# One transformer layer with eight experts: invert, broadcast and scale one half of the heads one step sooner on VectorE, in five passes

## The reference

```python
x = L0_attn_in_features
mod = (_silu(L0_c) @ L0_wmod).reshape(L0_c.shape[0], 6, 1, -1)
...
h = _layernorm(x, axis=-1) * (1 + ca) + sa
x = x + ga * _L0_attn_ref(h, ...)            # 16 heads, causal
h = _layernorm(x, axis=-1) * (1 + cb) + sb
x = x + gb * _L0_ffn_ref(h, ...)
# inside _L0_ffn_ref
p = jax.nn.softmax(att, axis=-1)             # 32 heads, no mask
o = jnp.einsum('bhqk,bkhd->bqhd', p, v).reshape(B, S, D) @ wo + x
h = jax.nn.gelu(jnp.einsum('metd,edf->metf', xe, w1) + b1[None, :, None, :], approximate=False)
y = jnp.einsum('metf,efd->metd', h, w2) + b2[None, :, None, :]
```

## Time and profile before

| | us |
|---|---|
| median of 3 runs | 1638.02 (1637.07 to 1643.39) |
| the profiled execution | 1635.07 |
| its span, first to last instruction | 1633.3 |
| PE busy | 1456.5 (89%) |
| DVE busy | 1181.6 (72%) |
| ACT busy | 997.7 (61%) |
| POOL busy | 528.7 (32%) |

### The profile page before, as it was taken

How to read it: one execution, slowest core, us unless ns; L and a number is a source line. 1 busy time by engine, 2 the same in 40 slices (tenths; PEclk the granted TensorE clock), 3 DMA queues, 4 the chain that set the end, 5 groups by cost and what they waited for, 6 DMA issues and landing times.

```text
span 1633.3 us, 29723 instructions
## 1 busy us (share of the span) xinstructions
PE 1456.5 (89%) x9637; PEld 614.1 (38%) x9637; DVE 1181.6 (72%) x2891; ACT 997.7 (61%) x2075; POOL 528.7 (32%) x1218
## 2 busy tenths in 40 slices
PE   6685879988999989999899989999899979998987
PEld 4232423333434334343334334343343424343425
DVE  6567589778687776868777786878778587867620
ACT  1152557755667656776567756676577756776761
POOL 4232335245342333414343243414243133312100
PEclk9698899999999999999999999999999999999999
DMA  6851434555344452645345362554336242533111
GB/s 188 211 131 40 130 108 138 125 148 160 92 145 127 135 135 85 185 123 164 95 122 167 95 177 82 164 148 147 89 100 193 76 109 63 161 93 86 60 59 65
DMA packets 158749, 200.96 MB, mean 123 GB/s; under 512 B 24640, under 2 KB 109952, under 8 KB 158600
## 3 DMA queue, kind: packets, MB, share of 16 engines
q1 hardware_dynamic: 152712, 194.69, 42.1%
q10 hardware_dynamic: 5888, 4.37, 1.0%
HBM read 122.25 MB, written 75.58 MB: 121 GB/s over the span
## 4 chain that ended last, share of the span: by engine, by line
PE 62%; DVE 12%; ACT 7%; DMA 6%; issue 6%; SPq 4%; POOL 2%; POOLq 0%; ACTq 0%; DVEq 0%
PE bank_out L1456 15%; PE bank_scores L1437 11%; PE bank_max L1407 8%; PE bank_side L1370 6%; PE bank_side L1540 5%; DVE neg_max L1681 5%; PE bank_side L1380 3%; PE bank_max L1524 3%; DMA q_stack<-max_parts 3%; ACT probs L1228 3%; PE bank_side L1505 2%; DVE bank_max L1678 2%; PE bank_side L1494 2%; PE bank_side L1524 2%; PE bank_scores L1524 2%
## 5 line engine op out<-in xcount | busy, mean ns | idle before, releaser
L1228 ACT ACTIVATE probs<-bank_scores 128x512 f32<-128x512 f32 (+3 forms) x1536 | 752.4, 543 | 334.0 <-PE bank_scores L1437 324.8
L1681 DVE TENSOR_REDUCE neg_max<-bank_max 128x1 f32<-128x512 f32 x1024 | 654.4, 683 | 123.8 <-PE bank_max L1407 120.6
L1407 PE MATMUL bank_max<-k_stack,q_stack 64*128 64x512 bf16 (+3 forms) x2048 | 318.2, 347 | 74.9 <-DVE neg_max L1681 39.6
L1456 PE MATMUL bank_out<-probs,v_tile 128*9 128x512 f32 (+4 forms) x3072 | 369.3, 553 | 7.1 <-ACT out_raw L1243 2.9
L1437 PE MATMUL bank_scores<-q_stack,k_stack 64*128 64x512 bf16 (+3 forms) x2048 | 318.0, 347 | 43.0 <-ACT probs L1228 34.6
L1678 DVE CUSTOM_DVE_ANT_0 bank_max<-bank_max,causal 128x384 f32<-128x384 f32 (+3 forms) x512 | 241.7, 514 | 113.5 <-PE bank_max L1407 111.2
L1437 PEld LDWEIGHTS bank_scores<-q_stack,k_stack 64*128 64x128 bf16 x2048 | 81.3, 93 | 367.7 <-issue 341.1
L1078 POOL CAST max_parts<-max_row 16x128 bf16<-16x128 f32 x96 | 28.0, 292 | 526.1 <-DVE max_row L1692 526.1
L1407 PEld LDWEIGHTS bank_max<-k_stack,q_stack 64*128 64x128 bf16 x2048 | 104.6, 95 | 159.8 <-issue 91.3
L1540 PE MATMUL bank_side<-w_out,hidden_T 128*128 128x256 f32 x512 | 141.4, 402 | 3.1 <-issue 1.1
L1096 POOL TENSOR_SCALAR_AFFINE_SELECT probs<-probs 128x512 f32<-128x512 f32 x128 | 81.3, 635 | 116.3 <-ACT probs L1228 116.2
(11 more groups left out here) (154 smaller groups left out, 1452.3 us busy)
## 6 DMA issues: line engine op xcount, KB each, us to landing
q_stack<-q_parts SPq DMA_DIRECT2D x124, 256.0 KB, 4.7
k_stack<-k_parts SPq DMA_DIRECT2D x122, 192.0 KB, 6.3
out_raw<-out_raw SPq DMA_DIRECT2D x70, 256.0 KB, 2.0
w_in<-in_L_ffn_w_dram SPq DMA_DIRECT2D x16, 1024.0 KB, 5.2
w_out<-in_L_ffn_w_dram SPq DMA_DIRECT2D x16, 1024.0 KB, 6.1
q_parts<-partsq SPq DMA_DIRECT2D x32, 384.0 KB, 3.1
k_parts<-partsk SPq DMA_DIRECT2D x32, 384.0 KB, 3.3
q_parts<-partsq SPq DMA_DIRECT2D x32, 256.0 KB, 3.2
```

The costliest lines, as they stand in the source:

```text
L1228: nc.scalar.activation(probs[s % 2][:, head_at(k), q0:S], region[bank][:, q0:S], ACT.Exp, scale=float(WIDTH[a]) ** -0.5).then_inc(drained[ ...
L1407: ins = pe.matmul(region[to][:, 0:keys], q_stack[buf][rows, at, qt * P:(qt + 1) * P], k_stack[buf][rows, at, 0:keys], start=(i == 0), stop ...
L1456: ins = pe.matmul(outb[32 * k:32 * k + WIDTH[a] + 1, q0:S], v_tile[a][:, kt, g * GROUP + k, :], probs[s % 2][:, k, q0:S], start=(kt == 0), ...
L1681: v.tensor_reduce(dst, region[bank], AX_X, ALU.max).then_inc(drained[bank], 1)
```

## The change

In `place_pass` alone, the times of the five items of the second half of the wide heads move: `invert` and `store_inverse` from step 45 to step 44 (slot 1), `load_inverse` from 47 to 46 (slot 3), and `scale_heads` from step 49, slot 3, to step 49, slot 1. `load_sums` stays at step 42. This holds for the passes n = 1 to 5; the first pass and the tail have their own tables, which stay.

```diff
     place_units(plan, first, (191, 231, 231, 243, 281), heads_items(n, 1, 0))
     place_units(plan, first, (271, 301, 301, 321, 351), heads_items(n + 2, 0, 0))
-    place_units(plan, first, (421, 451, 451, 473, 493), heads_items(n, 1, 1))
+    place_units(plan, first, (421, 441, 441, 463, 491), heads_items(n, 1, 1))
     place_units(plan, first, (71, 73), in_pieces("ffn_sum", e, 0))
```

## The result

| | before | after |
|---|---|---|
| median | 1639.65 us (1637.07 to 1643.39, 4 runs) | 1614.35 us (1612.44 to 1617.61, 4 runs) |
| profiled execution | 1635.07 us | 1615.65 us |
| its span | 1633.3 us | 1613.9 us |

The ratio is 0.9846, 95% interval 0.9818 to 0.9874: faster by 25.3 us in the medians and by 19.4 us between the two profiled executions. The forecast was 20.0 us less, 1618 us, with a range of 1607 to 1631.

A forecast was written before the change was run, and what follows sets the result against it. PE was taken as the bound, with DVE setting the end only where PE waits for it. Passes 1 to 4 at -4.55 us each (-18.2) and pass 5 at -1.8 gave -20.0 us: 1618 us, range 1607 to 1631.

The forecast's parts named there:

- The stall at the product: Second-half scaling product, long beside GpSimd's row: PE's wait goes, 3.85 us in four passes, 4.3 in the fifth, plus 1.5 clock.
- The sum: Passes 1 to 4 at -4.55 us each, pass 5 at -1.8 us, total -20.0 us.
- Rival 4: At the scaling product GpSimd's cast gets in first and the stall stays: +15 us, 1653; chance 7%.
- The reciprocal: Step 44: the earlier reciprocal waits 1.9 us for the sums; PE loses 2.0 us, in pass 5 2.5 us.
- the landing: Sums' DMA, awaited by the reciprocal: lands 5.5 us after issue in pass 2, 4.8 to 6.5 us in the others.
- The DMA wait at step 48: PE's wait for the maxima's DMA, passes 1 to 4: landing stays though issue is later, -1.2 us in the mean.
- Rival 3: Maxima's DMA at step 48 lands later along with its issue, on top of rival 2: -9.2 us, 1628.8; chance 14%.
- The clock: PE's half clock: +1.5 us behind the new reciprocal gap, -1.5 us behind the vanished step 48 wait in passes 1 to 4.
- rival 1: No half clock behind the new gap at the reciprocal: -27.5 us, 1610.5; chance 17%.
- rival 2: Half clock both behind the new reciprocal gap and still at step 48: -14 us, 1624; chance 13%.
- the inverse's side: Reciprocal gap, step 48 wait and their clocks: 0.8 us lost in each of four passes, 4.0 in pass 5, +7.2.
- product's side: Stall at the scaling product and its half clock: gain of 5.35 us in passes 1 to 4, 5.8 us in pass 5.

The follow-up runs named there:

- e1: Only the product scale_heads moved (493 to 491), the inverse left in place, against the kernel before: 1609.34 us, ratio 0.9817.
- r2: e1 run again on another chip, beside the change, against the kernel before: 1610.28 us, ratio 0.9803.
- e3: Kernel before with only GpSimd's six bias_part operations moved to step 0 of each pass (13 to 3): 1613.08 us, ratio 0.9842.
- e4: Kernel before with only bias_part's two gate products moved to step 0, its four sums left in place: 1631.30 us, ratio 0.9948.
- r1: The change itself once more, on another chip, against the kernel before: 1614.91 us, ratio 0.9842.
- e5: The change plus load_sums two slots sooner (step 41, slot 3), against the kernel before: 1618.12 us, ratio 0.9857.
- e2: Only invert, store and broadcast of the inverse moved sooner, the product left at 493, against the kernel before: 1645.52 us, ratio 1.0040.
- e7: The change plus the 1 MB expert weights' load moved from step 41 to step 47, against the kernel before: 1600.01 us, ratio 0.9765.

## Why the prediction was right

**The stall at the product: right, in mechanism and size.** The product is at 0.67 us in all five places, GpSimd's cast took 0.68, PE's 3.85 us waits are gone at these places and so is the half clock behind them. e1 gives it alone: 30 us in the medians (31 in r2). The sum had 5.35 x 4 + 5.8 = 27.2 us for it. The traces of e1 and r2 show less than that between the marks (19.6 and 22.8 us), so the size is borne out by the medians alone. e3 gives nearly the same by taking away the other party, so the cause is the meeting of the two and not the place in DVE's list, and e4 gives the dose. Rival 4 (GpSimd first) didn't come: DVE was ahead by 0.13 us, for which 0.1 had been worked out. The margin is thin, but it held in every pass, in r1, e1, r2 and e5 as well.

**How long the loser waits.** The Trainium skill, page "SBUF — State Buffer", section "SBUF: two separate sides", has the lock held for the whole instruction by whoever starts first. For who blocks whom the runs agree. For how long they show more: e4 (3.40 us) and before (4.76 us) have a product that waits for the last of a row of four or six, not for one instruction of 0.7 us.

**The reciprocal: right, a little too small.** I took 1.9 us of wait and 2.0 us for PE; it was 2.09 to 2.35 us in passes 1 to 4 and equally long for PE, and in pass 5 2.70 and 2.78 us for the 2.5. The term that was off is the landing. I took it 5.5 us after the issue; after the change it came 5.9 us behind it in pass 2. The line in the earlier trace rows was misread too: the profile gives no landing for L975, and this one is of L976, the outputs issued 0.6 us later, as are the 4.8 to 6.5 us for the other passes. The semaphore events of before put the landing of the sums at 5.5 us in pass 2, so the figure holds by luck, and at 5.7 to 5.8 us in the others, which fits that no wait came out as short as the prediction's 1.3 us.

**The DMA wait at step 48: right.** Counted from the mark of each pass, the maxima's DMA was issued 1.3 to 3.6 us later than before in passes 1 to 4 and landed, by the semaphore events, 0.5 us later in the mean (it took 2.8 to 3.1 us from its first issue, before 4.3 to 5.1). So the wait went. Rival 3 is out. e1 shows the other side: without the earlier reciprocal the wait is there, 1.5 us in pass 3.

**The clock: half right.** I had the half clock behind the new gap in all five passes. It was there in passes 1, 2 and 5, and not in 3 and 4; in r1's trace it was in 1, 2, 4 and 5. So the truth lies between the forecast and rival 1 (-27.5 us). By the table above passes 1 and 2 came out at -4.7 in the mean, where the forecast has -4.55, and passes 3 and 4 at -6.0, where rival 1 has -6.05. r1 says the same: its passes 1, 2 and 4 take 183.55 us in the mean and pass 3, without the half clock, 182.03. Both fit the 1.5 us for such a stretch, and the old one at step 48 did go, so rival 2 is out. Which gap would be followed by half clock was a guess.

**The sum.** -23.5 us between the marks for a forecast of -20.0: two passes without half clock make 3.0 of the 3.5 us. In r1's trace, with one such pass, it is -19.9. In the medians it is -25.3.

**The two sides of it.** The sum priced the inverse's side at 2.0 + 1.5 - 1.2 - 1.5 = +0.8 us in a pass, +7.2 us in all with the 4.0 of pass 5. e2 measured +6 and e1 against the change +5, though I had put +3 for e2 on record. So the 5.3 us by which the medians passed the forecast are a product's side 3 to 4 us larger than its 27.2, and an inverse's side 1 to 2 us smaller. Why the first is larger isn't shown.

## What to carry to other kernels

Where a short DVE operation over SBUF has one very long case, look at what GpSimd has queued beside it: the length is that of GpSimd's whole row to its end, and moving either party by a step takes it away. When a step is moved sooner, move what it waits for too, and ask which large transfer stands ahead of it in the queue; it is that one that should give way (e7), not the small one that should jump the queue (e5). If a change is made of two moves, time each alone: here one of them brought 30 us and the other cost 5, by the medians.

## What the runs showed of the hardware

- A DVE product of two SBUF operands wasn't admitted between back-to-back GpSimd operations: 0.67 us alone, 3.40 beside four, 4.76 beside six, each time ending 0.55 us behind the last one. DVE's reductions out of PSUM ran beside the same operations at their usual 1.28 us for two.
- Gaps of PE of nearly the same length are followed by half clock or not: 2.25, 2.36 and 2.78 us were, 2.18 and 2.10 us weren't in the kernel after; in r1's trace 2.59, 2.34, 2.27 and 3.24 us were and 2.36 us wasn't.
- A 1 MB load decided when a small one landed that was queued behind it: the sums took 5.5 to 5.9 us in the kernel after, and 2.1 to 2.9 us once the weights had been moved. With the small load put ahead of it, PE waited up to 3.46 us at another place.
- The start of the run, the same in all kernels here but for the place of GpSimd's row, scatters by 7 us from trace to trace (398.6 to 405.8 us). Two profiled executions should be compared between marks inside them.
